# First stage reordered, FFN0's products interleaved in two buffers, a fifth late key: a two-layer decoder kernel

## The reference

```python
x = x + _L0_xattn_ref(_layernorm(x), ctx_4096, x1_scale, x1_zp, x2_scale, x2_zp)     # attention 0
x = x + _L0_ffn_ref(_layernorm(x), w_gate, w_up, w_down)                              # FFN0
x = x + _L1_xattn_ref(_layernorm(x), ctx_4096, ctx_4096, mask, wq, wk, wv, wo, 0)     # attention 1
x = x + _L1_ffn_ref(_layernorm(x), gate_w, up_w, down_w, gate_scale, up_scale, down_scale)
```

## Time and profile before

| | |
|---|---|
| median of 3 runs | 699.43 us (698.53 to 700.01) |
| the profiled execution, its own time | 699.82 us |
| its span, first to last instruction | 698.0 us |
| mean granted TensorE clock | 0.995 |
| TensorE busy | 662.3 us, 95% |
| VectorE busy | 520.7 us, 75% |
| ScalarE busy | 344.5 us, 49% |
| GpSimd busy | 466.1 us, 67% |

### The profile page before, as it was taken

One profiled execution on the slowest core, in us unless ns is written; L12 is line 12 of the kernel. 1 busy time (PEld: TensorE's weight loads), 2 busy tenths in 40 slices (PEclk: granted clock), 3 DMA queues, 4 the chain that ended last, 5 costly groups with the idle time before them and its releaser, 6 DMA issues.

```text
span 698.0 us, 10807 instructions
## 1 busy us (share of the span) xinstructions
PE 662.3 (95%) x3000; PEld 488.2 (70%) x3004; DVE 520.7 (75%) x1027; ACT 344.5 (49%) x663; POOL 466.1 (67%) x430
## 2 busy tenths in 40 slices
PE   5999997698989999999999999999999999899997
PEld 2444443344667788888888888888888877788886
DVE  5977998787678888888888888888888886621113
ACT  2675215324475566665665765666656663121111
POOL 0767546262679779789788698698598477066661
PEclk9999999999999999999999999999999999999999
DMA  8989836811312141131221221222124012012321
GB/s 337 388 262 279 227 76 150 224 41 39 125 57 83 36 132 46 66 100 45 86 79 45 90 75 62 73 75 75 60 75 135 16 31 83 8 46 90 105 76 61
DMA packets 59195, 72.63 MB, mean 104 GB/s; under 512 B 23200, under 2 KB 31520, under 8 KB 58144
## 3 DMA queue, kind: packets, MB, share of 16 engines
q1 hardware_dynamic: 59168, 72.31, 33.3%
HBM read 58.00 MB, written 9.44 MB: 97 GB/s over the span
## 4 chain that ended last, share of the span: by engine, by line
PE 66%; DVE 16%; issue 7%; POOL 4%; ACT 3%; DMA 2%; SPq 1%; DVEq 0%; ACTq 0%; POOLq 0%
PE ps L651 15%; PE ps L653 14%; PE ps L652 14%; PE ps L719 10%; PE ps L684 6%; PE ps L526 2%; PE ps L580 2%; DVE ps L1452 1%; DVE f L1339 1%; DVE f_amax L1335 1%; PE ps L514 1%; DVE mx_raw L1321 1%; DVE mx_amax L1305 1%; PE ps L540 1%; DMA mx_raw<-in_mxw 1%
## 5 line engine op out<-in xcount | busy, mean ns | idle before, releaser
L1121 POOL TENSOR_SCALAR prob<-prob,rinv 128x512 f32<-128x512 f32 x128 | 90.0, 703 | 73.5 <-DVE rinv L1459 73.4
L968 ACT ACTIVATE prob<-ps,nmax 128x512 f32<-128x512 f32 x128 | 88.4, 691 | 96.8 <-DVE nmax L1452 96.5
L719 PE MATMUL ps<-xt,wq_sb 128*128 128x512 f32 x384 | 103.2, 393 | 4.3 <-DVE q_cos L1467 2.1
L979 ACT CAST pT<-ps 128x512 fp32r<-128x512 f32 x128 | 75.2, 588 | 53.4 <-PE ps L684 52.4
L1452 DVE CUSTOM_DVE_ANT_0 ps<-ps,mask_sb 128x512 f32<-128x512 f32 x128 | 87.8, 686 | 6.8 <-PE ps L653 6.6
L1473 DVE TENSOR_TENSOR pT<-ps,pT 128x512 fp32r<-128x512 f32 x128 | 86.3, 674 | 3.1 <-ACT pT L979 2.0
L719 PEld LDWEIGHTS ps<-xt,wq_sb 128*128 128x128 f32 x384 | 71.6, 188 | 22.5 <-issue 5.1
L684 PE MATMUL ps<-idf,prob 128*128 128x128 f32 x512 | 76.7, 272 | 0.4 <-POOL prob L1121 0.3
L684 PEld LDWEIGHTS ps<-idf,prob 128*128 128x128 f32 x512 | 63.8, 141 | 17.3 <-POOL prob L1121 1.7
L651 PE MATMUL ps<-pT,vt 128*128 128x512 f32 x128 | 61.1, 478 | 0.5 <-DVE pT L1473 0.5
L514 PE MATMUL ps<-ctxT,wk_sb 128*128 128x512 f32 x128 | 57.6, 594 | 1.4 <-ACT v_st L847 1.4
(11 more groups left out here) (173 smaller groups left out, 1544.7 us busy)
## 6 DMA issues: line engine op xcount, KB each, us to landing
mx_raw<-in_mxw SPq DMA_DIRECT2D x8, 1024.0 KB, 7.5
wq_raw<-in_wq SPq DMA_DIRECT2D x32, 256.0 KB, 3.1
wo_raw<-in_wo SPq DMA_DIRECT2D x32, 256.0 KB, 2.7
v_scr<-v_st SPq DMA_DIRECT2D x16, 256.0 KB, 4.7
k_scr<-k_st SPq DMA_DIRECT2D x16, 256.0 KB, 3.2
kr<-k_scr SPq DMA_DIRECT2D x16, 256.0 KB, 2.8
kr_swp<-k_scr SPq DMA_DIRECT2D x32, 128.0 KB, 3.3
vr<-v_scr SPq DMA_DIRECT2D x16, 256.0 KB, 3.5
```

Source lines behind the costliest of these rows:

```text
L719: last = mm(query_bank(H), wq_sb[:, par, l, k], xt[:, r, k], start=(n == 0), stop=(n == 11))
L968: nc.scalar.activation(prob[:, j], bank(j % 2), ACT.Exp, bias=nmax[:, j:j + 1], scale=-1.0, accum_out=rsum[:, j:j + 1]).then_inc(exps, 1)
L979: copy(pT[:, v % 2, 0, :, i * P:(i + 1) * P], bank(2 + i % 2).rearrange("p (k c) -> p k c", k=4)).then_inc(ph_ready, 1)
L1121: nc.gpsimd.tensor_scalar(prob[:, i], prob[:, i], rinv[:, i:i + 1], 1.0, ALU.mult, ALU.mult).then_inc(probs, 1)
```

## The change

- `LATE_KEYS` gets a fifth key, (5,1), at its head. TensorE does its first half between turning the rows and the first slice of FFN0, its second half inside tile 2 of FFN0.
- The l units move forward: both into step 3, one behind key (2,1), one behind value (4,1). `place` follows.
- SyncE's list is written out anew: chunk loads stand earlier among the stores, ropeK's load goes from the start to step 4, and `rows_turn` is one transfer of 2048 columns. For that `q1T` is laid out by row tile.
- ScalarE's list is written out anew: both lifts of a chunk stand close together and ahead of the context's scaling; scaling and rounding of the context are parted.
- VectorE does the rounds of chunk 6 ahead of the second layernorm, not behind it.
- GpSimd scales the quantised rows in two halves; TensorE waits for each and turns two row tiles at a time, and FFN0's first slice waits for the first half alone.
- FFN0's products go to two buffers in turn (`int0` and the memory of `xhat`). The first two products of tile t+1 stand behind the maximum of tile t, the third behind its scaling.

```diff
-    ([("k", 2, 1), ("v", 4, 0)], [("v", 4, 1)]),
+    ([("k", 2, 1), ("l", 0, 0), ("v", 4, 0)], [("v", 4, 1), ("l", 1, 0)]),
...
-    ([("v", 7, 1), ("k", 5, 0), ("k", 5, 1)], []),
+    ([("v", 7, 1), ("k", 5, 0)], []),
 )
-LATE_KEYS = ((6, 0), (6, 1), (7, 0), (7, 1))
-LATE_BANK = (6, 2, 1, 3)
+LATE_KEYS = ((5, 1), (6, 0), (6, 1), (7, 0), (7, 1))
+LATE_BANK = (3, 6, 2, 1, 3)
...
-            q1T = sb("q1T", [P, KD, TOK], BF16, a)
+            q1T = sb("q1T", [P, NT, KD, P], BF16, a)
...
-                for t in range(NT):
-                    sp.dma_start(q1T[:, :, t * P:(t + 1) * P], q1[:, t], transpose=True).then_inc(q1T_in, 16)
+                sp.dma_start(q1T[:].rearrange("p t k r -> p (t k) r"), q1[:].rearrange("p t d -> p (t d)"), transpose=True).then_inc(q1T_in, 16)
...
-            sp.dma_start(ropeK[:], rope_k).then_inc(rk_in, 16)
...
-            stores(STEPS[0][0])
+            stores(STEPS[0][0][:2])
             mx_load(NRAW)
+            stores(STEPS[0][0][2:])
             ctx_load(1)
             stores(STEPS[0][1])
...
+            k_load(2)
+            mx_load(4)
+            stores(STEPS[1][0][:1])
+            chunk_turn(0)
+            stores(STEPS[1][0][1:])
+            mx_load(5)
+            stores(STEPS[1][1])
+            rows_turn()
+            chunk_turn(1)
+            k_load(3)
+            stores(STEPS[2][0])
+            mx_load(6)
+            stores(STEPS[2][1])
+            chunk_turn(2)
+            stores(STEPS[3][0] + STEPS[3][1])
+            mx_load(7)
+            k_load(4)
+            sp.dma_start(ropeK[:], rope_k).then_inc(rk_in, 16)
+            chunk_turn(3)
...
+                if b == 0:
+                    pe.wait_ge(consts_ready, 2)
+                    pe.wait_ge(q1T_in, 16)
...
+                if n == 0:
+                    for i in range(2 * NI // MXT + 1):
+                        pe.wait_ge(WT_in[i], 16)
+                    pe.wait_ge(*keys_out(5, 0))
+                    pe.wait_ge(q1T_ready, 1)
+                if n == 1:
+                    pe.wait_ge(q1T_ready, 2)
...
+            late_keys(0, range(0, 2))
             gate_up(0)
             gate_up(1)
+            gate_up_slice(2, 0)
+            late_keys(0, range(2, 4))
+            gate_up_slice(2, 1)
+            gate_up_slice(2, 2)
             pe.wait_ge(mx_free, 2 * NFULL + 1)
             turn_inter(0)
-            gate_up(2)
+            gate_up(3)
             down(0)
             turn_inter(1)
-            gate_up(3)
             down(1)
             turn_inter(2)
...
+            copy_values(0, 1)
+            mx_lift(2, 0)
+            mx_lift(2, 1)
+            copy_values(1, 1)
+            context_scale(0)
+            copy_keys(1, 0)
+            context_round(0)
+            copy_keys(1, 1)
+            mx_lift(3, 0)
+            context_scale(1)
+            mx_lift(3, 1)
...
+            def rows_out(h):
+
+                pool.wait_ge(f6_clipped, 1)
+                n = HALF // BLK
+                tt(blocks(q1[:, 2 * h:2 * h + 2].rearrange("p t d -> p (t d)")), blocks(f6c[:, h * HALF:(h + 1) * HALF]),
+                   over(f6_e[:, 0, h * n:(h + 1) * n], n), ALU.mult).then_inc(q1_ready, 1)
...
-                mx_round(i, 0)
-                mx_round(i, 1)
+                if i != L0_AT + 2:
+                    mx_round(i, 0)
+                    mx_round(i, 1)
...
                 if i == L0_AT + 1:
+                    mx_round(i + 1, 0)
+                    mx_round(i + 1, 1)
                     dve.wait_ge(l0_done, NT)
                     layernorm()
...
+            def inter(t):
+
+                return int0[:] if t % 2 == 0 else rows(xhat[:])[:, 0:IPAD]
...
             def inter_quantise(t):
+
+                m = IPAD // BLK
                 dve.wait_ge(inter_ready, 3 * t + 3)
-                fp6(int0[:], IPAD, t + 1)
-                fp6_clip(IPAD, [(q1_ready, NT + 1), (intq_ready, t)])
+                chain(f6s, nc.vector.tensor_reduce(f6_amax[:, 0:m], blocks(inter(t)), AX.X, ALU.max, apply_absolute_value=True))
+                inter_product(t + 1, 0)
+                inter_product(t + 1, 1)
+                fp6_scale(inter(t), IPAD, t + 1)
+                inter_product(t + 1, 2)
+                fp6_clip(IPAD, [(q1_ready, NT + 2), (intq_ready, t)])
...
-            for t in range(2, NT):
-                inter_products(t)
                 inter_quantise(t)
                 add_down(t - 2)
```

More of the change, by code:

```diff
@@ L443, in _ @@
             wq_load(3, 1)
-            for i, b in LATE_KEYS[:3]:
+            for i, b in LATE_KEYS[:4]:
                 key_store(i, b)
@@ L508, in attention0 @@
                     for k in range(KD):
-                        last = mm(bank(n), q1T[:, k, (2 * b + t) * P:(2 * b + t + 1) * P], q2[:, 4 * b + k], start=(k == 0), stop=(k == KD - 1))
+                        last = mm(bank(n), q1T[:, 2 * b + t, k], q2[:, 4 * b + k], start=(k == 0), stop=(k == KD - 1))
                     last.then_inc(l0_sums, 1)
@@ L1093, in _ @@
                 if i == L0_AT + 1:
[L1094 removed]
+                    rows_out(0)
+                    rows_out(1)
             scale_out(NFULL)
```

181 lines of the change are left out of this document (94 added, 87 removed).

## The result

| | before | changed |
|---|---|---|
| median of the runs measured together | 698.98 us (698.49 to 700.01, 4 runs) | 692.5 us (691.27 to 693.55, 4 runs) |
| profiled execution: own time, span | 699.82, 698.0 us | 691.27, 689.7 us |
| first product of FFN0 on TensorE | 117.98 | 112.46 |
| int_q of row tile 3 | 156.83 (38.85 after FFN0's first product) | 150.79 (38.33 after it) |
| first query product | 173.66 | 167.63 |

The ratio is 0.9907 with an interval of 0.989 to 0.9923: 6.5 us faster, where 4.7 us were forecast (694.7, range 689.5 to 697.2).

A forecast was written before the change was run, and what follows sets the result against it. It took VectorE and TensorE as close rivals before about 172 us, TensorE as bound in the attention loop. First stage -5.1 and FFN0 +0.4 gave -4.7 us, forecasting 694.7, range 689.5 to 697.2.

The forecast's parts named there:

- VectorE's 8.33 us of idle time, less 2.7 of locks: First stage: all 8.33 us of VectorE's waits go, but it runs into GpSimd's last passes for 2.7 us.
- three stalls: VectorE's first-stage waits: 1.67 us for chunk 3's load, 3.10 for ScalarE's lift of chunk 2, 3.56 for chunk 5's load.
- The layernorm's lock, 4.6 to 0.3: Second layernorm: with chunk 6's rounds ahead, small VectorE operations' waits for GpSimd's passes shrink from 4.6 us to 0.3.
- 1.8 at 74.0: First stage: TensorE waits 1.8 us at 74.0 for VectorE to read attention 0's banks; FFN0's first product at 112.9.
- ScalarE's new order ends no wait of TensorE: First stage: beyond two named waits, ScalarE's reordering gains TensorE nothing, banks being asked for 10.3 us after filling.
- FFN0 gives back 0.4: FFN0's row tiles: 39.3 us from first product to int_q of tile 3, against 38.85 before.
- 13.6, +6.7, +8.8, +10.1: FFN0: tile 0's clip ends 13.6 us after the first product; tiles 1, 2 and 3 add the other times.
- the lock in tile 3: FFN0's tile 3: VectorE's operations wait for GpSimd's rope product and wq split, making the tile 10.1 us.
- 1.7 won by the clock in tile 0: FFN0's tile 0: half a key fills the 3.34 us gap, so the half clock's 1.7 us cost goes.
- Locks weaker: First stage and FFN0: VectorE gets in between GpSimd's instructions; gain of 6.5 to 11.7 us, say 690.5; chance 0.24.
- The clock falls again: Before tile 3's int_q TensorE waits about 3.6 us, then half clock costs 1.7 us: 696.4; chance 0.15.
- The slower rival: First stage: late loads plus locks hold TensorE at keys (3,1), first product at 121.2, 703.0 us; chance 0.09.

The follow-up runs named there:

- load5_late: The changed kernel with only weight chunk 5's load put back behind the turns of the rows and chunk 1 on SyncE's queue; median 697.27 us.
- short_pass: The changed kernel with GpSimd's second scaling pass of weight chunks 2 to 4 on 64 of 1024 columns; median 692.5 us, ratio 0.992.
- l_late: The changed kernel with both parts of attention 0 at their old places in TensorE's order; median 699.32 us, ratio 1.0022.
- norm_first: The changed kernel with VectorE's rounds of chunk 6 behind the second layernorm again; median 696.81 us, ratio 0.9985.
- serial_ffn0: The changed kernel with FFN0's row tiles one behind the other again, with one buffer; median 690.34 us, ratio 0.9919.
- ropes_late: The changed kernel with GpSimd's four rope products moved from FFN0 to behind the split of the second query weight; median 689.32 us, ratio 0.9857.
- short_rope: The changed kernel with GpSimd's four rope products in FFN0 on 16 of their 512 columns; median 690.34 us, ratio 0.9897.
- l1_between: The changed kernel with the second part of attention 0 one unit later, between keys (3,0) and (3,1); median 690.9 us, ratio 0.9898.
- four_late: The changed kernel with key (5,1) in the first stage again and only four late keys; median 694.83 us, ratio 0.9941.

## Why the prediction was right

Its sum was -5.1 in the first stage and +0.4 in FFN0. Measured to the first query product: -5.5 and -0.5, -6.0 in all. Of the 2.3 by which the spans differ besides, 1.9 is the clock at 600. The median of 692.5 lies in the range, but 2.2 us under 694.7 and so outside the 1.5 us around the forecast. The first stage came as worked out; FFN0 did not, and its error and the clock's both went to the fast side.

**VectorE's 8.33 us of idle time, less 2.7 of locks: right.** The column sums were forecast for 74.9 and are read at 74.50. load5_late shows what one of the three stalls is worth, and short_pass that the 2.7 us are waits for GpSimd's pass. The two other stalls, the single transfer for the turned rows and GpSimd's two halves have no run of their own: that they are worth what was forecast is read from the timeline alone.

**The layernorm's lock, 4.6 to 0.3: right, but not the whole of it.** 0.2 is left and the rows' clip starts at 99.11 (forecast 99.6). The trace has a lock that I did not list: beside GpSimd's scaling of the rows a clip takes 2.03 and an operation on 128x16 1.88. It cost nothing here: VectorE is idle for 3.43 us before its first product of FFN0, and done 1.2 us early with the bank that the late key wants. In l_late, with the same lock (2.02 and 1.88 us), it is some 3 us of the 4.20 that TensorE waits. And the rounds' new place mattered most for ScalarE's queue, which my steps do not contain (norm_first).

**TensorE: right.** The wait is 1.60 at 73.8 for 1.8 at 74.0, the first product at 112.46 for 112.9. The 0.4 between them is VectorE's, which had read the banks at 75.3 and not 75.8; from there TensorE's 37.1 us are as forecast. That "ScalarE's new order ends no wait of TensorE" is true of this order and rests on little: l_late used up the 1.2 us of room at the late key's bank, norm_first that of ScalarE's copies, and their first products came 3.7 and 3.6 us later.

**FFN0 gives back 0.4: the sign is wrong, the size is 0.9 off.** FFN0 was to be 0.4 us longer and is 0.5 shorter. By clip and clip the forecast was 13.6, +6.7, +8.8, +10.1. They end at 13.6, 20.4, 28.8 and 38.2: +6.8, +8.4, +9.4. The term mis-sized is the lock in tile 3. The order of the two engines' turns is the one forecast: a small operation behind int_q and behind each rope product, the scaling behind the copy, the subtraction behind the scaling, the clip behind the subtraction. The last small operation was done 5.5 us after tile 2's clip, as forecast. From there copy, scaling, subtraction and clip were to take 4.6 us and took 3.9: the copy ended at 6.1 (forecast 6.4), the scaling at 7.6 (8.1), the subtraction at 8.7 (9.3), the clip at 9.4 (10.1). These four came closer behind each other than I had them. In tile 2 the locks took 1.95 us for 2.2.

Taken apart, the forecast had 1.7 won by the clock in tile 0 and 2.1 lost by the new order. In serial_ffn0 tile 0's clip ends 10.9 us after the first product, for 12.6 before the change: 1.7, as forecast. The new order costs 0.8 against serial_ffn0 (38.33 to 37.50) and 1.2 against the kernel before less that 1.7 (38.85 - 1.7 = 37.15). So that the interleaving is a loss was in the forecast, and is shown; its size was 0.9 to 1.3 us too large, and this turned the sign of the sum.

The Trainium skill (SBUF — State Buffer, section Who interferes with whom) has the pair of ports as an exclusive lock for a whole instruction, and counts an operation with two SBUF inputs among its takers. This trace agrees: the scaling, which reads two, takes 1.98 beside GpSimd and 1.62 without, and GpSimd's subtraction 2.51 and 1.31.

**The rivals.** "Locks weaker" (690.5, 0.24) did not come, though 6.5 us is the near end of its gain: the traces have the locks whole. Its 34.0 us of row tiles is what ropes_late (34.02) and short_rope (34.29) come to, but partly by chance, for both still have locks in tile 3 and less work on GpSimd. "The clock falls again" before tile 3 is turned is not in the changed kernel's trace, where the gap is 2.43 us and not 3.6. Of seven traces with this gap (2.42 to 2.44) it is the only one without the fall. In l1_between came this:

```profile
153.50:156.80 3.30, 3.30 (x8) 0.78 (x7) 2.95 (x13) 1.09 (x1) 0.00 (x0) 0.50 0.02 5
```

It cost 1.05 us there (17.89 from int_q to the query product for 16.84), not 1.7. Three of the changed kernel's four runs have mean clocks of 0.998, 0.998 and 0.994 and took 1.2 to 2.3 us more than the traced one. So this rival is likely in the median of 692.5; where the clock fell in those runs is not shown, since they have no trace. The slower rival, TensorE held at the keys (3,1), is close to what load5_late made, though TensorE was held one part earlier, at the value (4,1): the mechanism is real, 4.2 us at the first product and 4.8 in the median, and the change keeps clear of it by that load's place.

## What to carry to other kernels

Before filling an engine's idle time, look what its neighbour does in it: here the gap of 1.5 us kept VectorE's small operations out of the way of GpSimd's products, and filling it was worth nothing until they were moved (-0.8 against +2.1 us). A read of a bank, a lift or a copy that nobody waits for today holds whatever is queued behind it: two moves that looked harmless, one on VectorE and one on TensorE, cost 3.6 us through ScalarE's queue and 3.7, clock included, through one bank. And compare stages trace with trace before medians, when a clock that falls or not moves every run by 1 to 2 us.

## What the hardware showed that I had not expected

- The same gap of TensorE is followed by half clock in one execution and not in another. The gap of 2.42 to 2.44 us before tile 3's turn was followed by it in six traces of seven (in four_late it began just before the gap ended), and the waits of 1.16 and 1.06 us around 600 in eight of fourteen. At 74 us waits of 1.37, 1.60, 1.65 and 1.76 had no fall, and 2.01, 2.08 and 2.27 had one.
- The half clock lasted from 66.3 to 73.1 us in load5_late, behind the gap of 3.07, twice as long as in the rows shown of the others.
- Its price depends on what stands there: 1.7 us for eight products of the keys, 0.8 to 1.05 at tile 3's turn, 1.4 to 1.9 in FFN1.
- Of the pair VectorE and GpSimd both can wait: two instructions of 1.62 and 1.31 took 1.98 and 2.51 side by side. A short operation pays most: 0.19 alone, 1.14 to 1.19 beside a product of 1.27, which took no longer for it.
